# Expert blocks of a mixture-of-experts loop with the weights stationary and the token rows moving

## The chip, the cores and the metric

One core of a Trainium2 chip runs the whole program. The metric is the device time of one execution in microseconds; three runs of the kernel before took 991.32, 992.77 and 993.33 us, median 992.77.

## The reference, cut to what matters

Two decoder layers work on 1,024 tokens of width 256. Each has an attention, a second mixing part and a feed-forward part, and a layer norm behind each. The change touches the feed-forward part of the first layer alone, a mixture of 64 experts with one shared expert that every token passes:

```python
E, K, H, F_EXP = (64, 6, 256, 176)
def _swiglu(x, g, v, o):
    return jax.nn.silu(x @ g) * (x @ v) @ o
scores = jax.nn.softmax(x @ w_router.T, axis=-1)
topw, topi = jax.lax.top_k(scores, K)
combine = jnp.zeros((T, E), x.dtype).at[jnp.arange(T)[:, None], topi].add(topw)
def body(acc, ws):
    g, v, o, cw = ws
    return (acc + cw[:, None] * _swiglu(x, g, v, o), None)
routed, _ = jax.lax.scan(body, jnp.zeros_like(x), (wg, wv, wo, combine.T))
shared = _swiglu(x, swg, swv, swo)
return (routed + shared).reshape(b, s, h)
```

Each token goes to six experts; an expert has 176 hidden units; g and v are 256 x 176, o is 176 x 256, all f32.

## The kernel before, in words

The kernel is written in five instruction streams, one for each engine, that are ordered by semaphores. The first 450 us are the first layer's attention and scan. Then comes routing (471 to 513 us in the profile): the router's logits, the top six of each token, the rank of each token within its expert, and from these a table of blocks. A block is 128 token rows of one expert. Block e is expert e's first 128 rows, for e from 0 to 63; what goes beyond is put into more blocks behind. The blocks are worked in groups of four (NJ). Groups 0 to 15 (FIXED) are always there and their experts are known, so their weights can be loaded ahead; how many more groups are used (one here, 17 in all) comes out of routing, and for these SyncE reads each block's expert number from memory.

In routing the shared expert is worked too, four token tiles of 128 rows at a time: gate and value product, tanh, two multiplies on VectorE, two transposes of the hidden values, ScalarE's copy of them, the down product, a copy into y_sh (lines 948 to 966, 1785 to 1817, 2307 to 2317). Its instructions stand in each engine's order between those of routing.

For a block of the loop the following is done.
- POOL gathers the block's 128 token rows of x from DRAM (an indirect DMA into xg, line 1479), as soon as the rows of the same place in the group before have been turned.
- TensorE turns xg by two transposes (line 1006); ScalarE copies the result into xgT.
- TensorE multiplies: xgT is the stationary operand (128 x 128, once for each half of the width), and the 352 gate and value columns of the expert move (line 948). Out come token rows by hidden units.
- ScalarE takes the tanh of half the gate; VectorE forms (tanh + 1) * gate and multiplies by the value (lines 2310, 2314), which is twice the wanted product.
- TensorE turns the 176 hidden columns in two halves of 88 (line 954), ScalarE copies them into hidT, and TensorE multiplies them with the down weights (line 960), hidT stationary, 256 columns moving.
- VectorE halves the result into y_out (line 2468), SyncE stores it into y_dram (line 651) and then loads the weights of the block two groups on into the place that has come free (lines 630 and 631).

Weights have room for two groups (RING = 2); xg, xgT, hidT and y_out have room for one. Every matmul with f32 operands shows in the trace as two instructions of the same shape, a transpose as one. TensorE's order in a group is: the gate/value products of blocks 0 to 3, with the turns of the hidden values of blocks 0 and 1 among them; then for each block the down product, the turn of the next group's gathered rows, and the turn of the hidden values two blocks on:

```python
for j in range(NJ):
    up_g(j)
    if j >= 2:
        turn_up(j - 2)
for j in range(NJ):
    down(i * NJ + (j + TILES), j, 2 * j + 1, lambda f: dn(j, f))
    turn_g(i + 1, j)
    if j + 2 < NJ:
        turn_up(j + 2)
```

SyncE's order is block by block: wait for the copy of block j, store it, load the weights for the same place. VectorE may overwrite a block's y_out when the store of that place, a group earlier, has landed (semaphore y_stored[j]). Between the expert work VectorE and ScalarE do pieces of the second layer's key preparation (rotate_key, rest, stack, pick_weights and others), one piece in each block's place.

After the loop POOL waits for all stores of y and gathers each token's six rows back from y_dram (line 1507), where slot_idx has the row numbers; VectorE adds them up with the weights of routing. Everything after that is the same in both kernels.

Of the kernel before, what the change touches and what calls it, by code (L numbers as in the profile page):

```python
# [16 lines left out]
P = 128  # L17
# [3 lines left out]
KD = D // P  # L21
# [12 lines left out]
FH = F // 2  # L34
FP = 96
# [99 lines left out]
ACT_STEPS = 1 + PAIRS + 1  # L135

# [18 lines left out]
def build(nc, a, out):  # L155

    with ExitStack() as ctx:
# [180 lines left out]
        g_th = sb("g_th", [P, NJ, F])  # L338
        hid = sb("hid", [P, NJ, F])
        hidT = sb("hidT", [FH, NJ, 2 * P])  # L340
        xg = sb("xg", [P, NJ, D])
        xgT = sb("xgT", [P, NJ, KD * P])
        sh_gv = sb("sh_gv", [P, KD, 2 * F])
        sh_dn = sb("sh_dn", [FH, 2, D])
# [133 lines left out]
        y_stored = [sem(f"y_stored{j}") for j in range(NJ)]  # L478
# [3 lines left out]
        gv_ready = sem("gv_ready")  # L482
        g_tanh = sem("g_tanh")
        g_silu = sem("g_silu")
        hid_ready = sem("hid_ready")
        hid_turned = sem("hid_turned")
        hidT_copied = sem("hidT_copied")
# [57 lines left out]
        def pair(n):  # L545
            return ps[:, n:n + 2, :].rearrange("p a b -> p (a b)")

# [6 lines left out]
        def _(sp):  # L554
# [69 lines left out]
            for dst, src in ((sh_gv, "sh_gv"), (sh_dn, "sh_dn"), (pos, "pos"), (ident_bf, "ident_bf"),  # L624
                             (x_wq, "x_wq"), (x_wo, "x_wo"), (head_sel, "head_sel")):
# [3 lines left out]
            def load_block(e, j, gv, dn):  # L629
                sp.dma_start(gv, a["w_gv"][bass.ds(e, 1)].rearrange("a p k n -> (a p) k n")).then_inc(w_loaded[j], 16)  # L630
                sp.dma_start(dn, a["w_dn"][bass.ds(e, 1)].rearrange("a p k n -> (a p) k n")).then_inc(w_loaded[j], 16)

            for r in range(RING):
                for j in range(NJ):
                    if r:
                        sp.wait_ge(w_loaded[j], 32 * r)
                    load_block(r * NJ + j, j, w_gv[:, r * NJ + j], w_dn[:, r * NJ + j])
# [25 lines left out]
            used = used_groups(sp)  # L663
            with sp.Fori(FIXED, used) as i:
                for j in range(NJ):
                    e = sp.value_load(expert_row[0:1, bass.ds(i * NJ + (j - E), 1)], min_val=0, max_val=E - 1)
                    buf = bass.ds((i & 1) * NJ + j, 1)
                    store_y(i - RING, j)
                    sp.wait_ge(w_loaded[j], at(i, 32, 0))
                    sp.sem_inc(load_due, 1)  # L670
                    load_block(e, j, w_gv[:, buf].rearrange("p a k n -> p (a k) n"),
                               w_dn[:, buf].rearrange("p a k n -> p (a k) n"))
            for r in range(RING):
                for j in range(NJ):
                    store_y(used - RING + r, j)
# [23 lines left out]
        def _(pe):  # L699
# [245 lines left out]
            def gate_up(j, x_of, w):  # L945

                for k in range(KD):
                    last = mm(ps[:, j, 0:2 * F], x_of(k), w(k), start=(k == 0), stop=(k == KD - 1))  # L948
                last.then_inc(gv_ready, 1)

            def turn_hid(n, j, bk):
                pe.wait_ge(hid_ready, n + 1)
                for f in range(2):
                    last = nc.tensor.transpose(ps[0:FH, bk, f * P:(f + 1) * P], hid[:, j, f * FH:(f + 1) * FH], ident[:])
                last.then_inc(hid_turned, 1)

            def down(n, j, bk, w):
                pe.wait_ge(hidT_copied, n + 1)
                for f in range(2):
                    last = mm(ps[:, bk, 256:512], hidT[:, j, f * P:(f + 1) * P], w(f), start=(f == 0), stop=(f == 1))  # L960
                last.then_inc(down_ready, 1)

            def shared_up(tiles):

                for t in tiles:
                    if t >= NJ:
                        pe.wait_ge(down_copied, t - NJ + 1)
                    gate_up(t % NJ, lambda k: xT[:, k, t * P:(t + 1) * P], lambda k: sh_gv[:, k, :])

            def shared_down(tiles):  # L970
                for t in tiles:
                    turn_hid(t, t % NJ, t % NJ)
                for t in tiles:
                    down(t, t % NJ, t % NJ, lambda f: sh_dn[:, f, :])

            pe.wait_ge(layer_loaded, 128)
            shared_up(range(NJ))
# [10 lines left out]
            shared_down(range(NJ))  # L988
            shared_up(range(NJ, TILES))
# [11 lines left out]
            shared_down(range(NJ, TILES))  # L1001

            def turn_g(i, j):
                pe.wait_ge(gathered[j], at(i, 16, 16))
                for k in range(KD):
                    last = nc.tensor.transpose(ps[:, 2 * j, k * P:(k + 1) * P], xg[:, j, k * P:(k + 1) * P], ident[:])  # L1006
                last.then_inc(xg_turned, 1)

            def group(i, gv, dn):
                def up_g(j):  # L1010
                    pe.wait_ge(xgT_copied, at(i, NJ, j + 1))
                    pe.wait_ge(w_loaded[j], at(i, 32, 32))
                    pe.wait_ge(down_copied, at(i, NJ, j + 1) + TILES - NJ)
                    gate_up(2 * j + 1, lambda k: xgT[:, j, k * P:(k + 1) * P], lambda k: gv(j, k))

                def turn_up(j):
                    turn_hid(i * NJ + (j + TILES), j, 2 * j + 1)

                for j in range(NJ):
                    up_g(j)  # L1020
                    if j >= 2:
                        turn_up(j - 2)
                for j in range(NJ):
                    down(i * NJ + (j + TILES), j, 2 * j + 1, lambda f: dn(j, f))
                    turn_g(i + 1, j)
                    if j + 2 < NJ:
                        turn_up(j + 2)

            pe.wait_ge(down_copied, TILES)
# [3 lines left out]
            with pe.Fori(0, FIXED // RING) as d:  # L1033
                for r in range(RING):
                    group(d * RING + r, lambda j, k: w_gv[:, r * NJ + j, k, :], lambda j, f: w_dn[0:FH, r * NJ + j, f, :])
            used = used_groups(pe)
            with pe.Fori(FIXED, used) as i:
                group(i, lambda j, k: w_gv[:, bass.ds((i & 1) * NJ + j, 1), k, :].rearrange("p a n -> p (a n)"),
                      lambda j, f: w_dn[0:FH, bass.ds((i & 1) * NJ + j, 1), f, :].rearrange("p a n -> p (a n)"))

# [4 lines left out]
            pe.wait_ge(down_copied, at(used, NJ, 0) + TILES)  # L1045
            pe.wait_ge(xgT_copied, at(used, NJ, NJ))
# [358 lines left out]
        def _(pool):  # L1405
# [54 lines left out]
            pool.wait_ge(layer_loaded, 128)  # L1460
# [39 lines left out]
            for j in range(NJ):  # L1500
                pool.wait_ge(y_stored[j], at(used, 16, 0))
# [81 lines left out]
        def _(act):  # L1583
# [201 lines left out]
            def g_tanh_of(n, j, bk):  # L1785
                act.wait_ge(gv_ready, n + 1)
                f(g_th[:, j, :], ps[:, bk, 0:F], ACT.Tanh, scale=0.5).then_inc(g_tanh, 1)

            def hidT_of(n, j, bk):
                act.wait_ge(hid_turned, n + 1)  # L1790
                f(hidT[:, j, :], ps[0:FH, bk, 0:2 * P], ACT.Copy).then_inc(hidT_copied, 1)
# [6 lines left out]
            for r in range(TILES // NJ):  # L1798
                for j in range(NJ):
                    g_tanh_of(r * NJ + j, j, j)  # L1800
                if r:
                    for t in range(1, TILES):
                        scale_hot(t)
                    act.wait_ge(angle, 8)
                    f(cos_sin[:], ang[:], ACT.Sin).then_inc(cos_sin_ready, 1)
                    act.wait_ge(route_mm, 3)
                    f(expert_row[:], ps[0:1, Y, 0:P], ACT.Copy).then_inc(route_act, 1)
                else:
# [1061 lines left out]
```

## Time and profile before

| | before |
|---|---|
| runs, us | 991.32, 992.77, 993.33 |
| span of the profiled execution (the page gives no other time of it), us | 985.7 |
| mean granted TensorE clock | 0.961 |
| TensorE busy | 870.2 us, 88% |
| VectorE busy | 720.6 us, 73% |
| ScalarE busy | 510.4 us, 52% |
| POOL busy | 407.1 us, 41% |
| bytes moved by DMA | 106.46 MB |

The span runs from the first to the last instruction. The shares are averages over stages with quite different limits: in the stage of the expert loop the DMA engines, which over the whole span move 108 GB/s, move about 310. A row of a timeline gives start, duration, engine, line, operation and shape of merged instructions, and in brackets the idle time before them. Matmuls are pipelined, so the step from one to the next is shorter than the duration of one. In rows of DMA issues the last figure is the median time from issue to landing.

### The profile page before, as it was taken

What the parts mean: (1) busy time and instruction counts of PE and PEld (TensorE: products, weight loads), DVE (VectorE), ACT (ScalarE), POOL (GpSimd) and SP (SyncE); (2) the same over time, 40 slices, a digit from 0 to 9 for tenths busy, and PEclk for the clock granted to TensorE, in tenths of its full rate; (3) what the DMA queues carried; (4) which work ended last, traced back from release to release, by engine and by line L of the source; (5) the groups of instructions that cost most, each with busy time, mean ns of one, the idle gap of its engine ahead of it and who ended that gap; (6) DMA issues with size and microseconds to landing.
All of it is one profiled execution on the core that took longest, in us unless ns stands there. A gap on an engine that the chain in (4) does not pass through costs nothing.

```text
span 985.7 us, 15418 instructions
## 1 busy us (share of the span) xinstructions
PE 870.2 (88%) x5267; PEld 568.3 (58%) x5271; DVE 720.6 (73%) x1377; ACT 510.4 (52%) x1022; POOL 407.1 (41%) x338
## 2 busy tenths in 40 slices
PE   7999999999999999988889999999546867899886
PEld 3466666666565666656666777677423654343443
DVE  5667786959696867768774556665467798998797
ACT  3563554545544444445444334455522457898485
POOL 0203448494848577534214333333377312221013
PEclk9999999999999999989999999999866998999998
DMA  5451212112131221100926999999633000000001
GB/s 189 153 196 27 65 49 86 70 65 77 58 102 53 81 75 65 44 1 1 238 94 216 298 311 310 313 312 303 179 96 98 26 1 3 5 8 6 1 6 38
DMA packets 54743, 106.46 MB, mean 108 GB/s; under 512 B 8909, under 2 KB 26645, under 8 KB 54165
## 3 DMA queue, kind: packets, MB, share of 16 engines
q1 hardware_dynamic: 48917, 89.88, 29.6%
q0 software_dynamic: 5760, 15.74, 6.0%
q8 instruction: 37, 0.61, 0.3%
q14 instruction: 29, 0.24, 0.1%
HBM read 88.45 MB, written 17.14 MB: 107 GB/s over the span
## 4 chain that ended last, share of the span: by engine, by line
PE 54%; DVE 19%; DMA 10%; issue 5%; ACT 5%; SPq 3%; POOL 3%; DVEq 0%; ACTq 0%; POOLq 0%
PE ps L777 10%; PE ps L715 6%; DMA w_dn<-in_w_dn 5%; PE ps L873 5%; PE ps L725 4%; DVE row_max L2696 3%; PE ps L948 3%; DMA y_dram<-y_out 3%; PE ps L1280 3%; POOL key_part L1507 2%; DVE state L2119 2%; PE ps L795 2%; PE ps L960 2%; DMA key_part<-y_dram,slot_idx 2%; PE ps L1266 2%
## 5 line engine op out<-in xcount | busy, mean ns | idle before, releaser
L1479 POOL DMA_INDIRECT xg<-x_dram,tok_of x68 | 65.1, 958 | 131.8 <-PE ps L1006 94.2
L777 PE MATMUL ps<-w_vg,xT 128*128 128x512 f32 x256 | 116.8, 597 | 1.2 <-DVE th L2162 1.2
L1429 POOL TENSOR_TENSOR state<-state,rows_bc 128x1024 f32<-128x1024 f32 x22 | 53.8, 2446 | 95.5 <-DVE state L2119 41.9
L715 PE MATMUL ps<-xT,w_qks 128*128 128x512 f32 x192 | 86.5, 596 | 5.2 <-ACT qT L1585 5.2
L948 PE MATMUL ps<-w_gv,xgT 128*128 128x352 f32 (+1 forms) x272 | 87.4, 464 | 2.5 <-DMA w_dn<-in_w_dn 2.4
L2696 DVE TENSOR_REDUCE row_max<-ps 128x4 f32<-128x1024 f32 x64 | 74.3, 1217 | 7.1 <-PE ps L1245 6.3
L2130 DVE TENSOR_TENSOR aT<-ps,tri 128x768 f32<-128x768 f32 x64 | 59.7, 954 | 27.0 <-PE ps L725 26.9
L1585 ACT ACTIVATE probT<-ps 128x512 f32<-128x512 f32 x128 | 69.5, 594 | 10.1 <-PE ps L1266 9.6
L777 PEld LDWEIGHTS ps<-w_vg,xT 128*128 128x128 f32 x256 | 45.8, 190 | 48.8 <-issue 43.1
L960 PE MATMUL ps<-w_dn,hidT 88*128 88x256 f32 (+1 forms) x272 | 70.0, 379 | 0.0
L948 PEld LDWEIGHTS ps<-w_gv,xgT 128*128 128x128 f32 x272 | 48.9, 190 | 27.0 <-issue 5.2
L715 PEld LDWEIGHTS ps<-xT,w_qks 128*128 128x128 f32 x192 | 34.9, 190 | 46.6 <-issue 36.4
L1422 POOL TENSOR_TENSOR drive<-du,rows_bc 128x1024 f32<-128x1024 f32 x26 | 61.0, 2361 | 0.1
L1585 ACT ACTIVATE v<-ps 128x256 f32<-128x256 f32 x64 | 24.5, 382 | 70.6 <-PE ps L777 70.3
L1507 POOL DMA_INDIRECT key_part<-y_dram,slot_idx x48 | 49.9, 1039 | 26.9 <-DMA y_dram<-y_out 12.6
L873 PE MATMUL ps<-w_o,oT 128*128 128x256 f32 x256 | 60.7, 386 | 0.3 <-DVE xres L2235 0.3
L2162 DVE SCALAR_TENSOR_TENSOR th<-th,ps 128x256 f32<-128x256 f32 x64 | 26.5, 417 | 44.7 <-ACT th L1585 44.0
L2468 DVE TENSOR_SCALAR y_out<-ps 128x256 f32<-128x256 f32 x68 | 28.7, 422 | 41.7 <-DMA y_dram<-y_out 26.7
L873 PEld LDWEIGHTS ps<-w_o,oT 128*128 128x128 f32 x256 | 48.1, 194 | 9.9 <-issue 4.2
L1433 POOL TENSOR_TENSOR y<-y,state 128x1024 f32<-128x1024 f32 x22 | 51.9, 2357 | 1.7
L1585 ACT ACTIVATE g_th<-ps 128x176 f32<-128x176 f32 x76 | 23.6, 317 | 54.6 <-PE ps L948 54.4
L2310 DVE SCALAR_TENSOR_TENSOR g_th<-g_th,ps 128x176 f32<-128x176 f32 x76 | 25.4, 335 | 35.5 <-ACT g_th L1585 34.7
(327 smaller groups left out, 2066.6 us busy)
## 6 DMA issues: line engine op xcount, KB each, us to landing
w_gv<-in_w_gv SPq DMA_DIRECT2D x68, 352.0 KB, 8.2
rows_bc<-x_dbl_dram SPq DMA_DIRECT2D x32, 512.0 KB, 3.8
w_dn<-in_w_dn SPq DMA_DIRECT2D x68, 192.0 KB, 9.6
y_dram<-y_out SPq DMA_DIRECT2D x68, 128.0 KB, 7.5
y_dram<-blank SPq DMA_DIRECT2D x4, 1408.0 KB, 13.2
w_vg<-in_wvg SPq DMA_DIRECT2D x8, 512.0 KB, 4.9
w_qks<-in_wqks SPq DMA_DIRECT2D x8, 384.0 KB, 3.1
w_o<-in_wo SPq DMA_DIRECT2D x8, 256.0 KB, 2.7
```

What stands on the lines that cost most here:

```text
L715: last = mm(bank(PJ + n % 2), w_qks[:, k, part * P:(part + 1) * P], xT[:, k, half * 512:(half + 1) * 512], start=(k == 0), stop=(k == KD - 1))
L777: last = mm(bank(PJ + t % 2), xT[:, k, t * P:(t + 1) * P], w_vg[:, k, :], start=(k == 0), stop=(k == KD - 1))
L873: last = mm(ps[:, X + b % 2, 256 * t:256 * t + 256], oT[:, h, c:c + P], w_o[:, h, :], start=(h == 0), stop=(h == 1))
L948: last = mm(ps[:, j, 0:2 * F], x_of(k), w(k), start=(k == 0), stop=(k == KD - 1))
L960: last = mm(ps[:, bk, 256:512], hidT[:, j, f * P:(f + 1) * P], w(f), start=(f == 0), stop=(f == 1))
L1422: G.tensor_tensor(drive_buf(m), du[:, e], b_row[:, n % 2], ALU.mult).then_inc(drive_ready, 1)
L1429: G.tensor_tensor(state_of(m), state_of(m), c_row[:, n % 2], ALU.mult).then_inc(read_out, 1)
L1479: G.indirect_dma_start(xg[:, j, :], None, x_dram, bass.IndirectOffsetOnAxis(ap=col, axis=0)).then_inc(gathered[j], 16)
L1507: G.indirect_dma_start(yg[:, n % 8, :], None, y_dram, bass.IndirectOffsetOnAxis(ap=slot_idx[:, n // TOPK, n % TOPK:n % TOPK + 1], axis=0)) ...
L1585: return nc.scalar.activation(out, in_, func, **kw)
L2130: return V.tensor_tensor(aT[:, 2 * b:2 * b + 2, :], ps[:, first_bank:first_bank + 2, 0:384], tri[:].unsqueeze(1).to_broadcast([P, 2, 384]) ...
L2696: V.tensor_reduce(row_max4[:, u, :, 4 * i + 2 * (b % 2):4 * i + 2 * (b % 2) + 2], src, AX.X, ALU.max).then_inc(unit_free, 1)
```

## The change

Gate and value products are turned: the expert's weights become stationary and the 128 token rows of a block move, so the hidden values come out with units on the partitions and tokens along the columns, as the down product needs them. The transposes of the hidden values and ScalarE's copies of them go. The 176 units are split into 112 (FA) and a rest of 64 (FB). For the 112, gate and value are products of their own; the rests of gate and value are one product with 128 columns of weights, gate in partitions 0 to 63 and value in 64 to 127. The multiply puts the rest of an even block into partitions 0 to 63 of hidT_b and that of an odd block into 64 to 127, and their down products, each over 64 rows, stand one behind the other into different banks. ScalarE's Silu takes the place of the tanh and one of VectorE's multiplies; the factor 0.5 goes.

The work of a group goes by pairs of blocks. All four down products are counted as one event; two VectorE copies take the four results (even and odd blocks), then SyncE stores each pair in one DMA with 2 KB for each partition (in y_dram the rows of a pair of blocks lie one in the other, and slot_idx is computed for that by four more operations) and loads the weights of the pair's blocks, three DMAs a block instead of two, without the 8 padded rows of w_dn. The two stores of group 15 are issued by ScalarE; the last stores stand inside the loop instead of behind it. VectorE's copies wait for both stores of the group before. rotate_key moves ahead of the copies. The shared expert is worked in the same turned form, 512 tokens at a time, its last multiplies now ahead of the table's end.

```diff
-        w_gv = sb("w_gv", [P, RING * NJ, KD, 2 * F])
-        w_dn = sb("w_dn", [FP, RING * NJ, 2, D])
+        w_up = sb("w_up", [P, RING * NJ, KD * UP])
+        w_dn = sb("w_dn", [FA, RING * NJ, D])
+        w_low = sb("w_low", [P, RING * NJ // 2, D])
...
+        def y_rows(i, p):
+            rows = y_dram[bass.ds(i * (NJ * P) + p * 2 * P, 2 * P), :]
+            return rows.rearrange("(r two) d -> r (two d)", two=2)
...
@@ SyncE
-            def store_y(i, j):
-                sp.wait_ge(down_copied, at(i, NJ, j + 1) + TILES)
+            def store_y(i, p):
+                sp.wait_ge(down_copied, at(i, 2, COPIED + 2))
                 sp.sem_inc(load_due, 1)
-                sp.dma_start(y_dram[bass.ds(i * (NJ * P) + j * P, P), :], y_out[:, j, :]).then_inc(y_stored[j], 16)
+                sp.dma_start(y_rows(i, p), y_pair(p)).then_inc(y_stored[p], 16)
             with sp.Fori(0, FIXED // RING - 1) as d:
                 for r in range(RING):
-                    for j in range(NJ):
-                        store_y(d * RING + r, j)
-                        sp.wait_ge(w_loaded[j], at(d, 32 * RING, 32 * (r + RING)))
-                        sp.sem_inc(load_due, 1)
-                        load_block(d * (RING * NJ) + ((r + RING) * NJ + j), j, w_gv[:, r * NJ + j], w_dn[:, r * NJ + j])
+                    for p in range(2):
+                        store_y(d * RING + r, p)
+                        for j in (2 * p, 2 * p + 1):
+                            sp.wait_ge(w_loaded[j], at(d, LOADS * RING, LOADS * (r + RING)))
+                            sp.sem_inc(load_due, 1)
+                            load_block(d * (RING * NJ) + ((r + RING) * NJ + j), j, r)
...
@@ TensorE
+                for p in range(2):
+                    pe.wait_ge(xgT_copied, at(i, 2, p + 1))
+                    pe.wait_ge(hid_ready, at(i, 4, HIDDEN - 4 + p + 1))
+                    for o in range(2):
+                        j = 2 * p + o
+                        pe.wait_ge(w_loaded[j], at(i, LOADS, LOADS))
+                        up(ps[0:FA, p, 2 * o * P:(2 * o + 1) * P], w_of(j), "gate", x_of(j))
+                        last = up(ps[0:FA, p, (2 * o + 1) * P:(2 * o + 2) * P], w_of(j), "value", x_of(j))
+                    last.then_inc(up_ready, 1)
+                for p in range(2):
+                    pe.wait_ge(hid_ready, at(i, 4, HIDDEN - 4 + 2 + p + 1))
+                    for o in range(2):
+                        last = up(ps[:, 2 + p, o * P:(o + 1) * P], w_of(2 * p + o), "low", x_of(2 * p + o))
+                    last.then_inc(up_ready, 1)
+                pe.wait_ge(down_copied, at(i, 2, COPIED))
+                for p in range(2):
+                    pe.wait_ge(hid_ready, at(i, 4, HIDDEN + p + 1))
+                    for o in range(2):
+                        mm(ps[:, 4 + o, p * D:(p + 1) * D], hidT_a[:, 2 * p + o, :], w_dn[:, r * NJ + 2 * p + o, :],
+                           start=(p == 0), stop=False, skip_group_check=True)
+                    for o in range(2):
+                        turn_g(i + 1, 2 * p + o)
+                for p in range(2):
+                    pe.wait_ge(hid_ready, at(i, 4, HIDDEN + 2 + p + 1))
+                    for o in range(2):
+                        rows = slice(HIGH * o, HIGH * o + FB)
+                        last = mm(ps[:, 4 + o, p * D:(p + 1) * D], hidT_b[rows, p, :], w_low[rows, r * (NJ // 2) + p, :],
+                                  start=False, stop=True, skip_group_check=True)
+                last.then_inc(down_ready, 1)
...
@@ ScalarE, one group
+                for p in range(2):
+                    act.wait_ge(up_ready, at(i, 4, HIDDEN + p + 1))
+                    f(silu_a[:, 2 * p:2 * p + 2, :], ps[0:FA, p, :].rearrange("p (e two n) -> p e two n", e=2, two=2)[:, :, 0, :],
+                      ACT.Silu).then_inc(silu_ready, 1)
...
@@ VectorE, one group
+                dve.wait_ge(down_ready, at(i, 1, 3))
+                if not first:
+                    for p in range(2):
+                        dve.wait_ge(y_stored[p], at(i, 16, 0))
+                for o in range(2):
+                    V.tensor_copy(y_out[:, o::2, :], bank(4 + o).rearrange("p (a d) -> p a d", a=2)).then_inc(down_copied, 1)
```

## Rows read from the trace of the kernel before

**Rows 1.** Windows by group: us; engines' busy times (PE to POOL); PEclk, DMA share, GB/s

```profile
521.27:531.33 10.06, 10.06 (x50) 7.61 (x50) 3.99 (x12) 5.24 (x14) 4.72 (x6) 1.00 0.32 86
...
582.14:592.64 10.50, 10.28 (x50) 7.43 (x49) 5.51 (x18) 4.00 (x12) 3.78 (x5) 1.00 1.06 317
...
676.74:687.42 10.68, 10.38 (x51) 7.44 (x49) 6.11 (x18) 5.92 (x18) 2.33 (x4) 1.00 1.05 290
```

**Rows 2.** DMA issues of 552 to 675 us

```profile
w_gv<-in_w_gv SPq DMA_DIRECT2D x46, 352.0 KB, 8.4
w_dn<-in_w_dn SPq DMA_DIRECT2D x46, 192.0 KB, 9.7
y_dram<-y_out SPq DMA_DIRECT2D x47, 128.0 KB, 8.2
```

**Rows 3.** Chain that ended last, 455 to 760 us: start, duration, what

```profile
574.02 9.40 DMA y_dram<-y_out
...
699.41 3.57 DMA y_dram<-y_out
```

**Rows 4.** Waits of 521 to 700 us: who for whom, us, times, longest

```profile
DVE y_out L2468 <- DMA y_dram<-y_out: 26.7, 19, 1.9
```

**Rows 5.** Timeline of TensorE, loop's first group

```profile
529.15 1.03 PE L960 MATMUL ps<-w_dn,hidT 88*128 88x256 f32 x4
530.02 0.38 PE L1006 MATMUL ps<-ident,xg 128*128 128x128 f32 x2
```

**Rows 6.** Timeline of TensorE in the attention, 57 to 59.8 us

```profile
56.91 0.39 PE L840 MATMUL ps<-v,aT 128*128 128x128 f32 x2
57.13 0.39 PE L841 MATMUL ps<-v,aT 128*128 128x128 f32 x2
57.45 0.92 PE L725 MATMUL ps<-wT,eT 64*128 64x256 f32 x8
58.30 0.49 PE L839 MATMUL ps<-v,aT 128*128 128x128 f32 x2
```

**Rows 7.** Timeline of SyncE's DMA issues, loop's first burst

```profile
528.28 0.36 SPq L651 DMA_DIRECT2D y_dram<-y_out  x1
...
530.32 0.37 SPq L651 DMA_DIRECT2D y_dram<-y_out  x1
...
534.01 0.36 SPq L651 DMA_DIRECT2D y_dram<-y_out  x1
...
535.17 0.35 SPq L631 DMA_DIRECT2D w_dn<-in_w_dn  x1
```

**Rows 8.** DMA issues at 528.28, 530.32, 534.01 and 535.17, one by one

```profile
y_dram<-y_out SPq DMA_DIRECT2D x1, 128.0 KB, 1.7
...
y_dram<-y_out SPq DMA_DIRECT2D x1, 128.0 KB, 5.5
...
y_dram<-y_out SPq DMA_DIRECT2D x1, 128.0 KB, 6.6
...
w_dn<-in_w_dn SPq DMA_DIRECT2D x1, 192.0 KB, 7.5
```

**Rows 9.** Groups by line and form, whole span

```profile
L2103 DVE TENSOR_SCALAR sT<-ps 128x512 f32<-128x512 f32 x16 | 10.3, 676 | 4.8 <-PE ps L715 4.8
...
L2468 DVE TENSOR_SCALAR y_out<-ps 128x256 f32<-128x256 f32 x68 | 28.7, 422 | 41.7 <-DMA y_dram<-y_out 26.7 <-PE ps L960 14.2
```

**Rows 10.** Timeline of routing, 469 to 523 us

```profile
479.23 5.00 PE L948 MATMUL ps<-sh_gv,xT 128*128 128x352 f32 x16 [0.71 <-DMA x_bo<-in_x_bo]
...
484.66 0.34 DVE L2310 SCALAR_TENSOR_TENSOR g_th<-g_th,ps 128x176 f32<-128x176 f32 x1
...
487.14 0.21 DVE L2367 TENSOR_SCALAR blocks<-ps 128x64 f32<-128x64 f32 x1
```

**Rows 11.** Timeline of SyncE, last group's loads

```profile
677.14 0.36 SPq L651 DMA_DIRECT2D y_dram<-y_out  x1
...
679.71 0.36 SPq L651 DMA_DIRECT2D y_dram<-y_out  x1
```

More of the change, by code:

```diff
@@ L943, in _, with part_of, up @@
             last.then_inc(route_mm, 1)
-            def gate_up(j, x_of, w):
+            def part_of(w, k, part):
+                first = k * UP + dict(gate=0, value=FA, low=2 * FA)[part]
+                return w[:, first:first + (2 * FB if part == "low" else FA)]
+            def up(out, w, part, x_of):
                 for k in range(KD):
[L948 to L960, printed above, removed]
-                last.then_inc(down_ready, 1)
[L963 to L977, printed above, removed]
+                    last = mm(out, part_of(w, k, part), x_of(k), start=(k == 0), stop=(k == KD - 1))
+                return last
+            Y_SH = (3, 2)
+            def shared_up(h):
+                def x_of(k):
+                    return xT[:, k, h * 512:(h + 1) * 512]
+                if h:
+                    pe.wait_ge(hid_ready, 2)
+                up(ps[0:FA, 0, :], sh_up, "gate", x_of)
+                up(ps[0:FA, 1, :], sh_up, "value", x_of).then_inc(up_ready, 1)
+                if h:
+                    pe.wait_ge(down_copied, 2)
+                up(bank(2), sh_up, "low", x_of).then_inc(up_ready, 1)
@@ new lines, in shared_down @@
+            def shared_down(h):
+                pe.wait_ge(hid_ready, 2 * h + 1)
+                if h:
+                    pe.wait_ge(down_copied, 2)
+                for t in (0, 1):
+                    mm(ps[:, Y_SH[0], t * D:(t + 1) * D], hidT_a[:, t, :], sh_dn[:], start=(t == 0),
+                       stop=False, skip_group_check=True)
+                pe.wait_ge(hid_ready, 2 * h + 2)
+                for t in (0, 1):
+                    mm(ps[:, Y_SH[1], t * D:(t + 1) * D], hidT_a[:, 2 + t, :], sh_dn[:], start=(t == 0),
+                       stop=False, skip_group_check=True)
+                for t in (0, 1):
+                    for n in range(2):
+                        rows = slice(HIGH * n, HIGH * n + FB)
+                        last = mm(ps[:, Y_SH[n], t * D:(t + 1) * D], hidT_b[rows, t, :], sh_low[rows, :], start=False,
+                                  stop=True, skip_group_check=True)
+                last.then_inc(down_ready, 1)
@@ L1005, in turn_g @@
                 for k in range(KD):
-                    last = nc.tensor.transpose(ps[:, 2 * j, k * P:(k + 1) * P], xg[:, j, k * P:(k + 1) * P], ident[:])
+                    last = nc.tensor.transpose(ps[:, 6 + j // 2, (j % 2) * D + k * P:(j % 2) * D + (k + 1) * P],
+                                               xg[:, j, k * P:(k + 1) * P], ident[:])
                 last.then_inc(xg_turned, 1)
[L1009 to L1027, printed above, removed]
@@ L1818, in xgT_of @@
-            def xgT_of(i, j, first):
-                act.wait_ge(xg_turned, at(i, NJ, j + 1))
+            nc.scalar.preload_act_table_set("silu_and_others")
+            silu_shared(0)
+            scale_probs()
+            keep_shared(0)
+            scale_hot(0)
+            silu_shared(1)
+            for t in range(1, TILES):
+                scale_hot(t)
+            act.wait_ge(angle, 8)
+            f(cos_sin[:], ang[:], ACT.Sin).then_inc(cos_sin_ready, 1)
+            act.wait_ge(route_mm, 3)
@@ L1840, in cast_key @@
+                for p in range(2):
+                    act.wait_ge(up_ready, at(i, 4, HIDDEN + 2 + p + 1))
+                    f(silu_b[HIGH:P, 2 * p:2 * p + 2, :].rearrange("p a b -> p (a b)"),
+                      ps[0:FB, 2 + p, 0:2 * P], ACT.Silu).then_inc(silu_ready, 1)
+                for p in range(2):
+                    xgT_of(i + 1, p)
+                if side:
+                    side(2)
+                    side(3)
             def cast_key(j, q):
@@ L1857, in stack_key @@
                     last.then_inc(stacked, 1)
-            for j in range(NJ):
-                xgT_of(0, j, True)
+            for p in range(2):
+                xgT_of(0, p, True)
             for i in range(FIXED):
@@ L2362, in _ @@
                                         in1=far_base[:].unsqueeze(1).to_broadcast([P, TILES, E]), op0=ALU.mult, op1=ALU.add))
-            for j in range(NJ):
-                hidden(j, j, j)
+            hidden_shared(0, 0)
+            hidden_shared(0, 1)
             dve.wait_ge(route_mm, 2)
```

236 lines of the change are left out of this document (123 added, 113 removed).

## The prediction

> **What bounds the kernel now.** The page comes first: TensorE is its busiest engine, so shorter matmuls look like a gain. The change touches only routing's shared expert and the loop over 17 groups of four expert blocks, so I then read the loop group by group, in windows cut where a group's first gate matmul starts [rows 1]. It runs from 521.27 to the issue of its last y store at 699.41 [rows 3], 178.1 us. Its first groups take 10.0 with TensorE busy throughout; from 582.14 to 687.42 ten groups take 105.3, 10.53 each, with holes on TensorE and a DMA share of 1.05 to 1.06. The issues of this stretch say what a group moves [rows 2]: a block's weights are 352 + 192 KB, its y 128 KB, its gather by the code 128 rows of 1 KB. Four blocks are 3,200 KB, 3.28 MB; over 10.53 us that is 311 GB/s, the rate that the windows show. Landings of 8 to 10 us after issue say the same: a full queue. The chain of waits runs through one of these landings in most of these groups, such as a y store of 9.40 [rows 3], and VectorE waits 26.7 us in all, 19 times, for a y store before it may overwrite y_out [rows 4]. So after the first groups the DMA queue and the reuse of buffers bound the loop; TensorE is a near second.
>
> **TensorE, part by part.** A f32 matmul is two instructions, a transpose one. Starts give the step of one instruction: four with 256 moving columns take 0.87 to the next line's start, 0.217 each [rows 5]; pairs of 128 columns, each instruction with a new 128-column weight, start 0.22 apart, 0.11 each [rows 6], so the weight loads of the turned form stay hidden. A group before is 10.0 [rows 1]. After: gate, value and rest are 48 x 0.11 = 5.3; down of the 112 units 8 x 0.217 = 1.7; eight transposes of gathered rows 0.9; the eight hid transposes go. The rests' downs take 4 x 0.217 = 0.9 if pairs run side by side. Eight 64-row instructions (four of 256, four of 128 columns) took 0.85 from their start to the next line's; one after the other they need 4 x 0.217 + 4 x 0.11 = 1.31; and entering that form cost 0.1, since the pair before it took 0.32 instead of 0.22 [rows 6]. With 0.2 for in and out the group is 9.0, so 1.0 less. This counts only where TensorE ends last: between 0 and 17 x 1.0. I count it for group 0 alone, because the transfers are late next.
>
> **The transfers.** Weights go from 544 to 352 + 112 + 64 = 528 KB a block (no padded rows); y and gathers keep their bytes. A group is 3.21 MB, 10.33 us at 311 GB/s: 0.2 less. What moves is when they are issued. Before, each block's y is copied, stored and its weights reloaded as soon as its own down product ends: the first store is issued at 528.28, 7.0 after the loop's start [rows 7]. After, all four blocks end together and two copies of 512 columns follow, 0.68 each as for another 512-column read of PSUM [rows 9], 1.5 with handoffs. So the first store and reload come at 9.0 + 1.5 = 10.5, 3.5 later, and then in a burst: store, six loads, store, six loads. SP takes 1.16 from a store to the second load after it and 1.85 a round of store and two loads [rows 7], so 0.69 from a load to the next store, and I take 0.55 for each further load: the second store is issued 1.16 + 4 x 0.55 + 0.69 = 4.05 behind the first, the last load about 8 behind.
>
> Two loops now close over a whole group.
> Stores: the next copies wait until both stores have landed, and the second stands behind two blocks' loads. In the loop's first burst, on an empty queue, the store behind one block landed at 530.32 + 5.5 = 535.8 and the one behind three at 534.01 + 6.6 = 540.6 [rows 7, 8]. Two blocks ahead is between, 538.2, so 9.9 after the burst's first issue. With the copies' 1.4 and 0.35 for handoffs (my allowance) the loop is 11.65.
> Weights, over two groups: that burst's last load landed at 535.17 + 7.5 = 542.7 [rows 7, 8], 14.4 after its first issue, 14.65 with a handoff. The last block's gate and value (0.9), all rests (1.8), downs, turns and rests' downs (3.7) and copies (1.5) follow: 22.5, or 11.25 a group.
> If the queue never empties, its work alone counts: 10.33. So the new period lies between 10.33 and 11.65. I take 10.95, the middle: what is left in the queue at a group's end, and the gathers, cover a part of the burst's start, but not all. Nothing hides this: TensorE's 9.0 ends sooner.
>
> The empty queue's first store landed 1.7 after its issue, the same 128 KB behind one block 5.5 [rows 8]; so here the place in the queue decides. The Trainium skill ("DMA: Bandwidth & Descriptors", section "Anatomy of one DMA — SWDGE (gpsimd) path") gives a DMA a fixed 2.0 us plus bytes / 436e3. By that alone the second store would land 2.6 us after its issue (an estimate from that page), and the store loop would not bind. By that rule the first would land in 2.3 us; it bears the rule out, the second does not.
>
> **Other engines.** ScalarE: four Silu of 256 columns and two copies of 512 take the place of twelve short instructions; VectorE: six multiplies and two copies, of twelve. ScalarE is busy 4.0 and VectorE 5.5 of a window of 10.5 [rows 1]; they stay hidden, or cost up to 0.3 a group where a key step stands ahead of the copies (I take 0). [...] POOL's gathers are issued a little later in the group and needed a group on: 0.
>
> **Routing.** VectorE's eight short products, from 484.66 to the block counts at 487.14 [rows 10], stand ahead of the chain to the first gather, 2.5; three take their place, 0.68 + 2 x 0.42 = 1.5 [rows 9]. Against that the shared gate product, 5.00 on TensorE before [rows 10], becomes 12 instructions of 512 columns (twice 0.217 each, 5.2) and waits for one load more (up to 0.5, an allowance), and the rank products follow it. Bounds: 1.0 gained, 0.7 lost; I take 0.45 gained, since VectorE, not TensorE, ends last there now. The four extra index operations run while VectorE waits for TensorE: 0.
>
> **The end.** For group 16 SP reads each expert's number: 2.57 between two stores [rows 11] instead of 1.85. Its loads are issued within 1.5 + 4 x 2.57 = 11.8 after group 14's copies and land about 4 later (between 1.7 [rows 8] and 9.7 [rows 2], near the low end as little is queued); 7.85 follow, 23.4 in all with no other handoff, where two periods are 21.9. The last store landed 3.57 after its issue [rows 3]; two of 256 KB take 0.8 more.
>
> **Sum.** To the last store's issue: 10.5 + 14 x 10.95 + 23.4 + 0.25 = 187.4 against 178.1: 9.3 more. Routing -0.45, the last store +0.8: +9.65. Of the profiled execution the page gives the span, 985.7; the 7.1 us between it and the median of the runs, 992.77, are taken as unchanged. So 985.7 + 9.65 + 7.1 = 1002.4; forecast 1002.
>
> **Rivals.** (1) Faster: the queue itself gets quicker. y goes out in rows of 2 KB instead of 1 KB and the padding is gone; if the mixture then moves at 325 GB/s (one window has 317 [rows 1]) the period is 9.9 and the end 22.4: 10.5 + 138.6 + 22.4 + 0.25 = 171.8, with the other two terms 6 less, 987. It decides from a period under 10.3. Against it: more, smaller loads in a group, and stores that wait. Its extreme is a loop bound by TensorE, 9.0 a group, some 25 us less; a DMA share of 1.06 speaks against that. (2) No change: the queue never empties, 10.33 a group: 10.5 + 144.6 + 23.4 + 0.25 = 178.8, +1 with the other terms, 994. For it: the queue was full before. By the fixed cost that the Trainium skill gives (the section named above) it would come out so. (3) The store loop in full, 11.65: 10.5 + 163.1 + 23.4 + 0.25 = 197.3, +19.5, 1012. (4) The rests don't run side by side: 0.9 more on TensorE, felt only in the weights loop, at most 0.45 a group, +6 on the forecast, 1008; the 64-row instructions speak against it [rows 6].
>
> **How the numbers follow.** Forecast, a period of 10.6 to 11.3 (997 to 1007): 0.48. Rivals 3 and 4: 0.17. Rival 2 (990 to 997): 0.17. Rival 1: 0.18. Two microseconds, 0.2%, are about what a measurement of this kernel can tell from no change. Faster by more: rival 1 and a little of 2, 0.22; within it 0.12, the middle of 2; slower 0.66. The range 988 to 1014 leaves out the far ends of rivals 1 and 3; the forecast's own range is 997 to 1007.
>
> **What would show it.** Right: the first reload issued near 531, groups starting some 10.9 apart from the second on, VectorE's copies waiting for a y store in nearly every group, TensorE waiting for loads inside groups, under 305 GB/s. Routing right: the first gather 0.3 to 0.6 earlier. Wrong: starts 10.4 apart or less with the DMA share still at 1.06 (rivals 2 and 1); over 9.5 of TensorE in group 0 (the step of 0.11 or the pairs); the second store landing within 3 us of its issue.

## The result, and the profile of the changed kernel

The changed kernel takes 1012.92 us (median of 4 runs, 1005.07 to 1016.87) against 992.05 for the kernel before. The ratio of the fast runs is 1.0247, with a 95% interval of 1.0201 to 1.0294, where the two medians alone would give 1.021. It is slower, as forecast, but by 20.9 us instead of 9.65. The two profiled executions lie further apart, 1013.7 and 985.7 in span; what follows explains that pair, 28.0 us.

All of it lies in the loop over the groups. That ran from 521.27 to 699.41, 178.1 us; now it runs from 521.49 to the issue of its last y store at 728.10, 206.6.

Windows by group (the columns of [rows 1]): a first group, a short one, the long one behind it, two stretches of the long one, and the same work as in the first of these two in another long group, group 6.

```profile
521.49:531.30 9.81, 9.81 (x73) 8.96 (x72) 3.40 (x12) 3.31 (x7) 3.83 (x4) 0.92 0.19 53
555.11:564.24 9.13, 9.13 (x74) 8.28 (x72) 4.68 (x14) 2.72 (x6) 3.86 (x5) 1.00 0.82 232
564.24:578.65 14.41, 11.40 (x74) 10.08 (x72) 4.59 (x14) 2.71 (x6) 3.86 (x5) 0.88 1.00 303
570.50:574.88 4.38, 4.38 (x24) 4.38 (x25) 0.89 (x3) 0.76 (x2) 0.00 (x0) 0.61 1.00 312
574.88:578.65 3.77, 3.77 (x26) 2.91 (x24) 2.08 (x9) 1.57 (x3) 1.94 (x2) 1.00 0.91 270
593.60:596.36 2.76, 2.76 (x25) 2.76 (x26) 0.71 (x2) 0.76 (x2) 0.00 (x0) 1.00 1.07 321
```

The even 10.5 of [rows 1] is gone: short groups (9.13, TensorE busy throughout) alternate with long ones (12.33 to 14.75, and 16.39 for group 14), 23.5 a pair around here. TensorE's own work is the 9.13; the rest of a long group is waiting, and a stretch at clock 0.61. Six of the seven long groups up to group 14 have such a stretch (clock 0.50 to 0.65); in group 6 the clock stays at 1.00. TensorE's timeline in the long group:

```profile
564.24 2.14 PE L977 MATMUL ps<-xgT,w_up 128*112 128x128 f32 x16
568.49 1.10 PE L977 MATMUL ps<-xgT,w_up 128*112 128x128 f32 x8 [2.10 <-DMA w_low<-in_w_low]
570.50 4.55 PE L977 MATMUL ps<-xgT,w_up 128*112 128x128 f32 x24 [0.91 <-DMA w_low<-in_w_low]
574.88 1.03 PE L1075 MATMUL ps<-w_dn,hidT_a 112*128 112x256 f32 x4
...
578.65 1.56 PE L977 MATMUL ps<-xgT,w_up 128*112 128x128 f32 x12
```

Blocks 2 and 3 wait for the last of their three loads. After the second wait 24 instructions take 4.38, 0.18 each, where the first 16 took 2.14, 0.13 each. The chain of waits from there (start, duration, what) shows who is late:

```profile
564.67 5.78 DMA w_low<-in_w_low
570.50 4.55 PE ps L977 x24
...
577.55 1.27 issue
578.82 1.30 DVE y_out L2546 x2
...
580.35 0.36 SPq L671
```

That load was the last of SyncE's burst, which began with a store 7.86 us earlier:

```profile
556.81 0.37 SPq L671 DMA_DIRECT2D y_dram<-y_out  x1
...
561.18 0.37 SPq L671 DMA_DIRECT2D y_dram<-y_out  x1
...
564.67 0.47 SPq L649 DMA_DIRECT2D w_low<-in_w_low  x1
```

From one such burst (556.81) to the next but one (580.35) is a closed cycle of two groups: 13.69 until the last load is in and block 3 starts, 4.38 for its products and the rests, 3.77 for downs, turns and rests' downs, 1.70 for copies and handoffs, 23.54.

Landings show that the queue is no longer full (552 to 675 us, beside [rows 2]); each burst meets a queue that has run down.

```profile
w_up<-in_w_up SPq DMA_DIRECT2D x41, 352.0 KB, 4.1
y_dram<-y_out SPq DMA_DIRECT2D x21, 256.0 KB, 2.9
w_dn<-in_w_dn SPq DMA_DIRECT2D x41, 112.0 KB, 4.3
w_low<-in_w_low SPq DMA_DIRECT2D x42, 64.0 KB, 5.0
```

The waits of 521 to 728 us (beside [rows 4]): the load's wait has become the large one, the store's has shrunk to 7 times, each in a short group.

```profile
PE ps L977 <- DMA w_low<-in_w_low: 28.8, 20, 3.6
...
DVE y_out L2546 <- DMA y_dram<-y_out: 17.4, 7, 3.4
```

At the loop's end (beside [rows 11]) SyncE issues group 16's loads from 700.89 to 709.88; TensorE waits 3.61 for the last of them:

```profile
712.70 1.10 PE L977 MATMUL ps<-xgT,w_up 128*112 128x128 f32 x8 [2.10 <-DMA w_low<-in_w_low]
717.41 4.64 PE L977 MATMUL ps<-xgT,w_up 128*112 128x128 f32 x24 [3.61 <-DMA w_low<-in_w_low]
```

### The profile page after: what moved, and what is told of

It is laid out like the page before. It is cut to its first block, busy times and chain, and to the rows that moved or that the text cites. A ratio compares the mean times of both kernels' runs of the same rounds, so it can differ in the third digit from the quotient of the medians.

```text
span 1013.7 us, 15833 instructions
## 1 busy us (share of the span) xinstructions
PE 871.4 (86%) x5651; PEld 592.9 (58%) x5655; DVE 705.6 (70%) x1303; ACT 484.2 (48%) x900; POOL 407.2 (40%) x338
## 4 chain that ended last, share of the span: by engine, by line
PE 54%; DVE 19%; DMA 7%; issue 6%; SPq 5%; ACT 5%; POOL 4%; DVEq 0%; ACTq 0%; POOLq 0%
PE ps L801 10%; PE ps L739 6%; DMA w_low<-in_w_low 5%; PE ps L897 5%; PE ps L749 4%; PE ps L977 4%; POOL key_part L1564 3%; DVE row_max L2776 3%; PE ps L1337 2%; DVE state L2181 2%; PE ps L819 2%; PE ps L1323 2%; PE ps L1075 2%; SPq L649 1%; PE ps L1302 1%
## 5 line engine op out<-in xcount | busy, mean ns | idle before, releaser
L977 PE MATMUL ps<-xgT,w_up 128*112 128x128 f32 (+1 forms) x816 | 112.2, 299 | 29.0 <-DMA w_low<-in_w_low 28.8
L977 PEld LDWEIGHTS ps<-xgT,w_up 128*112 128x112 f32 (+1 forms) x816 | 104.8, 202 | 38.7 <-DMA w_low<-in_w_low 16.9
L2529 DVE TENSOR_TENSOR hidT_a<-silu_a,ps 112x256 f32<-112x256 f32 x34 | 14.3, 419 | 71.8 <-ACT silu_a L1642 71.8
L1642 ACT ACTIVATE silu_a<-ps 112x256 f32<-112x256 f32 (+1 forms) x36 | 14.2, 395 | 90.4 <-PE ps L977 90.4
L2546 DVE COPY y_out<-ps 128x512 f32<-128x512 f32 x34 | 21.9, 686 | 31.9 <-DMA y_dram<-y_out 17.4
L2181 DVE TENSOR_TENSOR_SCAN state<-decay,drive 128x1024 f32<-128x1024 f32 x18 | 40.7, 2276 | 0.0
```

The source lines that it names most:

```text
L977: last = mm(out, part_of(w, k, part), x_of(k), start=(k == 0), stop=(k == KD - 1))
L1642: return nc.scalar.activation(out, in_, func, **kw)
L2181: V.tensor_tensor_scan(state_of(m), decay[:, m % 2], drive_buf(m), 0.0, ALU.mult, ALU.add).then_inc(scanned, 1)
```

## The experiments

Ratios are to the kernel before, measured on the same chip (987.8 to 988.9 us in these runs). "Loop" is from the first gate product to the issue of the last y store of the profiled run.

**The store loop or the weights loop?** (a_y_two) y_out is held twice, so no copy waits for the stores of the group just before.

```
-        y_out = sb("y_out", [P, NJ, D])
+        y_out = sb("y_out", [P, RING * NJ, D])
...
-                        dve.wait_ge(y_stored[p], at(i, 16, 0))
+                        dve.wait_ge(y_stored[2 * r + p], stored)
```

> The changed kernel with y_out held twice (groups of even and odd number write different halves, each with its own stored-semaphores), so that copies wait for the stores of two groups ago. Theory W (the two-group weights loop sets the period: burst's first issue, 13.4 us until the last load has landed, 4.4 for the last block's products at the low clock, 3.9 for the downs, 1.7 for the copies, 23.5 a pair of groups): VectorE's waits for y stores (17.4 us in 7 groups) go, but they stand in the short groups only, and the time stays within 3 us of the changed kernel's 1012.9. Theory S (my rival 3, the store loop): the period falls from 11.8 towards 10.5 and the time by 12 us or more.

Measured: 1014.09, ratio 1.0261 (1.0211 to 1.0311); loop 204.5. No wait of VectorE for a store is left among the waits; TensorE's wait for loads stands as it was:

```profile
PE ps L978 <- DMA w_low<-in_w_low: 26.4, 21, 3.7
```

The store loop, my rival 3, is out as the bound.

**The same loads, but waited for later** (a_split)**.** Gate and value wait for w_up alone, the downs for w_dn and w_low.

```
-                        pe.wait_ge(w_loaded[j], at(i, LOADS, LOADS))
+                        pe.wait_ge(up_loaded[j], at(i, 16, 16))
...
                     for o in range(2):
+                        pe.wait_ge(w_loaded[2 * p + o], at(i, LOADS, LOADS))
```

> The changed kernel with separate semaphores: gate and value wait for w_up alone, the down products for w_dn and w_low; no load is issued at another time. The last block's w_up is issued 1.05 us before its w_low and lands about 2 earlier. Theory W: the pair of groups gets 1.5 to 2.3 shorter, the kernel 10 to 18 us faster. Theory S or a queue that is slower by itself: within 3 us of 1012.9.

Measured: 999.48, ratio 1.0113 (1.0066 to 1.0160); loop 191.6, 15 less. Nothing leaves earlier and nothing is smaller; only the place of one wait moved. TensorE now waits for w_up, and no longer for w_low:

```profile
PE ps L989 <- DMA w_up<-in_w_up: 22.7, 19, 3.6
...
DVE y_out L2559 <- DMA y_dram<-y_out: 10.7, 8, 2.8
```

**Part of the burst issued earlier** (a_up_early)**.** Besides, SyncE reloads a pair's w_up once its rests are multiplied.

```
+                        sp.wait_ge(up_ready, at(d, 4 * RING, 4 * r + HIDDEN + 2 + p + 1))
+                        for j in (2 * p, 2 * p + 1):
...
+                            load_up(d * (RING * NJ) + ((r + RING) * NJ + j), j, r)
                     for p in range(2):
                         store_y(d * RING + r, p)
```

> As a_split, and SyncE reloads a pair's w_up as soon as that pair's rests are multiplied, some 5 us before the group's copies; stores, w_dn and w_low follow the copies as before. Two thirds of the weights so leave the burst. Theory W: no stall inside groups, the period falls to what the queue's work takes, 10.3 to 10.6 (at most 311 GB/s as before), so 990 to 996, near the kernel before. If the new mixture of transfers is slower by itself (under 290 GB/s whatever its order): a period over 11.1 and 1002 or more.

Measured: 990.8, ratio 1.0030 (1.0004 to 1.0056); loop 176.7, 30 less than the changed kernel's. The time is as expected, the period better: 9.57 over groups 2 to 14. The transfers of 560 to 660 us, and the wait that is left:

```profile
DMA packets 19560, 33.18 MB, mean 332 GB/s; under 512 B 2973, under 2 KB 10305, under 8 KB 19558
```

```profile
DVE y_out L2563 <- DMA y_dram<-y_out: 44.4, 13, 5.2
```

The kernel before, in the same stretch and also at a full queue:

```profile
DMA packets 16948, 31.06 MB, mean 311 GB/s; under 512 B 2420, under 2 KB 7253, under 8 KB 16944
```

The Trainium skill ("DMA: Bandwidth & Descriptors", section "Rules for kernel authors") advises to issue a DMA early and to wait on its semaphore late; these two runs are the two halves of that rule, the late wait worth 15 us of loop and the early issue another 15. In the run times they are 13 and 9 us: in its profile a_up_early's loop begins 3.1 us later than a_split's.

**The clock in the loop** (a_fill, and again a_fill2 beside the unchanged a_again)**.** TensorE gets more to do: six f32 products a group, results unused, ahead of the waits of blocks 2 and 3.

```
+                        for _ in range((0, 0, 2, 4)[j]):
+                            mm(ps[:, 2, 3 * P:4 * P], ident[:], ident[:], start=True, stop=True)
                         pe.wait_ge(w_loaded[j], at(i, LOADS, LOADS))
```

> The changed kernel with six more f32 matmuls of 128 columns a group on TensorE, results unused: two before the wait for block 2's weights and four before that for block 3's, 1.3 us of work a group by 0.109 us an instruction. They stand where TensorE waits anyway (3.4 us in each long group). Theory C (part of W: the wait lowers TensorE's clock, and block 3's products and the rests then run at 0.213 instead of 0.109 us an instruction, 1.7 us in each of 8 long groups): the granted clock stays near 1.0 over the stretch after the wait, that stretch falls from 4.3 to about 2.6, and the kernel gets faster by 6 to 14 us although it does more. If the clock is no part of the loop: no change within 3 us. If TensorE's work bounds the loop: 15 to 22 us slower.

Measured: 1006.06, ratio 1.0191 (1.0138 to 1.0244), an interval that overlaps the changed kernel's. So both ran again, side by side:

> The changed kernel itself once more, to have it beside a_fill2 on one chip: about 1013 again, 2.0 to 2.9% over the kernel before, and in a second profile the same pattern of long and short groups, 23 to 24 us a pair, the last block's gate and value and the rests at half the clock in the long ones.

> a_fill once more (six more f32 matmuls a group in TensorE's waits), because its interval, 1.0138 to 1.0244, overlapped that of the changed kernel. Theory C: 5 to 10 us under a_again, intervals apart. Without the clock in the loop: within 3 us of a_again.

Measured: the changed kernel 1016.03, ratio 1.0248 (1.0199 to 1.0297), with the same alternation; with the added products 1001.58, ratio 1.0139 (1.0109 to 1.0169). More work, and by the ratios 11 us less (14 by the medians), just beyond the 5 to 10 expected; the intervals lie apart. TensorE in a longer group of the first of the two runs, and a window over its last stretch:

```profile
560.15 1.13 PE L977 MATMUL ps<-xgT,w_up 128*112 128x128 f32 x8 [0.41 <-DMA w_low<-in_w_low]
561.11 1.06 PE L1063 MATMUL ps<-ident 128*128 128x128 f32 x8
562.12 2.91 PE L977 MATMUL ps<-xgT,w_up 128*112 128x128 f32 x24
```

```profile
562.12:564.87 2.75, 2.75 (x25) 2.75 (x25) 0.70 (x2) 0.76 (x2) 0.00 (x0) 1.00 1.05 332
```

The 24 instructions that took 4.38 at clock 0.61 take 2.75 at 1.00: 1.6 us that stood on the cycle of 23.54. The filling took the place of idle time; groups now take 10.48 (9.14 and the added 1.3) where nothing is late.

**The burst without the turned products** (b_burst)**.** In the kernel before, stores and reloads of a group are held until its fourth copy.

```
-                sp.wait_ge(down_copied, at(i, NJ, j + 1) + TILES)
+                sp.wait_ge(down_copied, at(i, NJ, NJ) + TILES)
```

> The kernel before with one change: SyncE's stores and reloads of a group all wait until its fourth block is copied, so they leave in one burst as in the changed kernel; matmuls and loads stay. Theory W (release in a burst is what costs): first issue some 5.7 us later, then a two-group loop of about 13.5 us from the first issue to the last load landed and 7.5 from the last block's gate to its copies, plus up to 1.7 for the low clock after the wait: 10.5 to 11.4 a group, 997 to 1010 against some 989 for the kernel before. Rival (the turned products or their twelve loads a group cost it, not the burst): within 3 us of the kernel before.

Measured: 1004.6, ratio 1.0205 (1.0148 to 1.0261); loop 195.6, period 11.31. One line of issue order costs 17 us, with the products of the kernel before: 17.4 us of loop, where the whole change costs 28.5. Which wait closes the cycle differs from my account, though: here the stores' is the larger one (waits of 521 to 717 us), and the rate of 560 to 660 us falls.

```profile
DVE y_out L2468 <- DMA y_dram<-y_out: 39.4, 26, 2.8
PE ps L948 <- DMA w_dn<-in_w_dn: 8.3, 11, 1.3
```

```profile
DMA packets 15695, 28.75 MB, mean 287 GB/s; under 512 B 2253, under 2 KB 6733, under 8 KB 15691
```

**What bounded the kernel before?** (b_two) y_out held twice there. SyncE itself now waits for the last store of the same place before it issues the next.

```
-        y_out = sb("y_out", [P, NJ, D])
+        y_out = sb("y_out", [P, RING * NJ, D])
...
-                    V.tensor_scalar(y_out[:, j, :], ps[:, 2 * j + 1, 256:512], 0.5, None, ALU.mult).then_inc(down_copied, 1)
+                    V.tensor_scalar(y_out[:, r * NJ + j, :], ps[:, 2 * j + 1, 256:512], 0.5, None, ALU.mult).then_inc(down_copied, 1)
```

> The kernel before with y_out held twice, so that copies wait for the stores of two groups ago; matmuls, loads and their order stay. My prediction read the kernel before as bound by the DMA queue's work (3.28 MB a group at 311 GB/s, 10.5 us), with the waits for y stores as its sign. If so: no change, within 3 us, the waits stand at the weights instead. If the 311 was no limit of the queue (a_up_early moved 332 GB/s) and the reuse of y_out was the bound: the period falls from 10.4 towards TensorE's 9.95 to 10.1 and the kernel by 4 to 8 us, the rate rises over 320 GB/s.

Measured: 987.97, ratio 0.9997 (0.9969 to 1.0024). VectorE's store wait of [rows 4] falls from 26.7 to 0.7, SyncE's new one (waits of 521 to 705 us) takes 1.7, and the rate stays:

```profile
DVE y_out L2473 <- DMA y_dram<-y_out: 0.7, 1, 0.7
SPq L655 <- DMA y_dram<-y_out: 1.7, 2, 1.5
```

```profile
DMA packets 16860, 30.81 MB, mean 308 GB/s; under 512 B 2406, under 2 KB 7232, under 8 KB 16856
```

So the prediction read the kernel before rightly: in this order of issue its queue is full at about 310 GB/s, and the reuse of y_out is not a bound of its own.

**Why does a full queue move more in a_up_early?** (a_y1k) Its y rows go back from 2 KB to 1 KB, and slot_idx needs four operations less.

```
-            return rows.rearrange("(r two) d -> r (two d)", two=2)
+            return rows.rearrange("(two r) d -> r two d", two=2)
```

> a_up_early with y stored block by block in rows of 1 KB, as the kernel before did, instead of two blocks' rows side by side, 2 KB. a_up_early's queue moved 336 GB/s at a DMA share of 1.05, the kernel before 311 at the same share. If the longer rows make that difference (my rival 1): the period goes from 9.6 back to 10.0 or more, 997 to 1002. If not: within 3 us of a_up_early's 990.8, and the 311 was not the queue's limit for other reasons.

Measured: 993.84, ratio 1.0083 (1.0050 to 1.0117), 3 us over a_up_early by the medians, 5 by the ratios, with intervals that just touch; period 9.85, not 10.0 or more:

```profile
DMA packets 21121, 31.86 MB, mean 319 GB/s; under 512 B 2835, under 2 KB 14719, under 8 KB 21119
```

An effect of the row length is not shown: a_over, below, has 2 KB rows and the loop of a_up_early up to group 13, and its period is 9.87. Nor does the mixture alone make the difference. The same stretch in the kernel before, a_split, a_up_early and a_over (the last two figures are DMA share and GB/s):

```profile
560.00:660.00 100.00, 97.17 (x456) 70.70 (x454) 61.34 (x173) 44.25 (x127) 36.44 (x39) 1.00 1.06 311
560.00:660.00 100.00, 89.43 (x680) 79.08 (x681) 53.11 (x133) 31.52 (x69) 36.13 (x38) 1.00 1.03 301
560.00:660.00 100.00, 96.96 (x750) 86.43 (x749) 56.50 (x143) 36.38 (x78) 41.87 (x43) 1.00 1.04 332
560.00:660.00 100.00, 96.85 (x751) 86.64 (x750) 57.41 (x145) 35.94 (x78) 39.83 (x41) 1.00 1.01 320
```

a_split moves the same transfers as a_up_early, in the changed kernel's order, and at a share of 1.03 they come to 301 GB/s, less than in the kernel before. So the order of issue matters too. What in the order does it, and what the rest of the mixture adds (no padded rows, smaller loads), was not tried.

**The end of the loop, and a version that beats both** (a_over, a_best)**.** Group 16's loads are split in the same way, and ScalarE stores group 14's y; then y_out is held twice as well.

```
+            sp.wait_ge(up_ready, 4 * (FIXED - 2) + HIDDEN + 4)
             with sp.Fori(FIXED, used) as i:
...
+                    load_up(e, j, 0)
+                sp.wait_ge(down_copied, 2 * (FIXED - 2) + COPIED + 2)
...
+                    load_down(experts[j], j, 0)
```

> As a_up_early, and the last group's w_up is reloaded behind group 14's rests too, its w_dn and w_low behind group 14's copies, ahead of no store of SyncE's (ScalarE issues group 14's y stores, as it did group 15's). In a_up_early group 16 still stalled, 18.7 us from its first gate to the last store's issue, and group 15 12.2. If late loads are the end's cause (W): these two fall to about 11 each and 10, 6 to 9 us less than a_up_early's 990.8, so 982 to 985. If the end is set by the gathers or the copies: within 2 us of it.

> As a_over with y_out held twice: copies wait for the stores of two groups ago. In a_up_early VectorE's copies waited 44.4 us for y stores in 13 groups and in four groups TensorE then waited for VectorE's hidT_a. If that store loop is what is left (S after W is gone): a mean period under 9.4 and 3 to 6 us less than a_over, 976 to 982. If the queue's work, 336 GB/s at a_up_early's 9.55 us a group, is the bound: the same as a_over within 2 us, the waits standing at the loads instead.

Measured: 984.0, ratio 0.9961 (0.9936 to 0.9986), and with y_out held twice 980.73, ratio 0.9917 (0.9884 to 0.9951); the two intervals overlap, so what the second step adds is not shown. In the first, group 16 starts with short waits where a_up_early waited up to 2.99:

```profile
686.09 1.10 PE L993 MATMUL ps<-xgT,w_up 128*112 128x128 f32 x8 [0.34 <-DMA w_up<-in_w_up]
687.88 2.91 PE L993 MATMUL ps<-xgT,w_up 128*112 128x128 f32 x24 [0.69 <-DMA w_up<-in_w_up]
```

The second waits neither for weights nor for stores; the gathers are next, and the period of groups 2 to 14 is 9.81, not the 9.4 expected:

```profile
PE ps L1061 <- DMA xg<-x_dram,tok_of: 7.9, 7, 2.1
```

## Why the prediction was wrong in size

By its own steps, in the profiled pair:

- **The bound before**: right (b_two).
- **TensorE**: right. A group without waits takes 9.13 for a predicted 9.0; steps are 0.109 and 0.215; the rests' pairs start 0.007 apart, and eight take 1.13, so rival 4 is out. Only group 0 is 9.81: it begins at the lower clock level, 0.92 in the mean of its window.
- **The burst**: nearly right. Second store 4.37 behind the first for 4.05, last load 7.86 behind for 8 (the prediction's own steps add up to 7.4); first issue 11.53 into the loop for 10.5. The second store landed some 4.8 after its issue (561.18 to the copies at 565.94), for the prediction's 5.9 (9.9 less 4.05), and not the 2.6 of the formula that it weighs. In the section that it names, the Trainium skill gives that formula for DMAs that GpSimd issues; these are SyncE's, and the kernel before's first one took 1.7 where the formula gives 2.3.
- **Store loop**: wrong as a bound. From one burst's first issue over the stores to the next it measured 10.66 (556.81 to 567.47) for 11.65, less than half of 23.54. Copies wait for a store in 7 groups, not in nearly all, and taking the wait away changed nothing.
- **Weights loop**: the right cycle, sized 22.5 for a measured 23.54. Its landing was 1.0 quicker (13.69 for 14.65), the rest within 0.3. **The step that failed** is its term for the last block's gate and value (0.9) and all rests (1.8): they took 4.38, not 2.7. I had costed the stall as waiting time only, and not that the products behind it run at the lower clock level; that is 0.84 a group. With products at full speed this cycle would have been 21.86, or 10.93 a group. Group 6 shows one: its products kept clock 1.00, and from group 4's copies to its own it took 21.47 (578.82 to 600.29).
- **The period of 10.95** was taken by a second wrong step: "I take 10.95, the middle: what is left in the queue at a group's end, and the gathers, cover a part of the burst's start, but not all." The weights loop is a chain in which each part waits for the one before. By the prediction's own figures it needs 11.25 a group, and no mean with the queue's 10.33 was to be taken; that is 0.3 too little. The quicker landing took back 0.48, which the forecast had not worked out, so that 10.95 lies next to 10.93 is luck. From group 0's copies (531.49) to group 14's (697.17) the period was 11.83, 0.88 more than forecast: 0.3 for the middle, 0.84 for the clock, less 0.48 for the landing, 0.14 for downs and copies, and pairs that were on average a little longer than the one above. Over 14 periods that is 12.4 us.
- **The end**: 28.8 from group 14's copies to group 16's for 23.4, 5.4 more. Group 16's last load lands 7.5 after its issue for my 4, with ScalarE's two stores and four gathers issued around it, and 1.7 goes to the clock again (0.60 from 717.41 to 721.89).
- **Other engines, routing**: within their bounds. VectorE's three shared products and their gaps take 1.61 (484.83 to 486.44) for 1.5, the first gather comes 0.35 earlier for 0.3 to 0.6. The loop's start, 519.9 to 525.1 in the profiles of these kernels, differs by more than that, so the gain in routing is not shown.

First issue 1.0, periods 12.4 and end 5.4 are 18.8 of the 19.2 by which the loop missed its forecast of 187.4. This is the profiled pair, which misses the forecast by 18.4; the medians miss it by 11.2. The profiled execution of the changed kernel took 1015.55, 2.6 over its median. That of the kernel before took some 987.6 (an estimate: time lies about 1.9 over the span in every other run here), 4.5 under its median, so most of the 7.1 that the forecast carried over was only this.

The 1.7 is the stall's second price. In the trace TensorE waits 2.10 and, after 1.1 of work, 0.91; of the 24 instructions behind, 15 then start 0.213 apart, as at 1.2 GHz; 0.109 is the step at 2.4. The Trainium skill ("TensorE: Matmul & The Clock Gate", section "HAM oscillation — how this bites in real kernels") tells of a loop that starts each step cold because it waits for a DMA; the trace agrees (0.61 behind the waits, 1.00 in a short group), and a_fill2 shows what it costs. It is not so behind every wait: in group 6 TensorE waits 1.65 and, after as much work, 1.07, and the clock stays at 1.00.

The figure of rival 3, 1012, came out by luck, not by its store loop. The faster queue of rival 1 was real but out of reach of this order of issue: it shows at 332 GB/s once the burst is broken up, and gives 9.57 a group, where rival 1 had 9.9 at 325.

## What to carry over

When a change lets buffers go all at once instead of one by one, add up the closed cycle from release to release; if that exceeds the queue's and the engine's work, it is the period, and no mean with the others is to be taken. Ask of each stall on TensorE whether the clock falls behind it: here it cost its length and, in all long groups but one, the products behind it at a granted clock of 0.50 to 0.65. Waiting only where data is used, and releasing each buffer at its last use, recovered all of the loss here: 980.7 with the same products, 987.8 for the kernel before beside it.

## What the runs showed of the hardware that I had not expected

- Work added into TensorE's waits made the kernel faster, 1.0139 for 1.0248 of the time before, because the granted clock behind them stayed up (1.00 instead of 0.61 in the windows above; 0.98 for 0.94 from 521.5 to 700 us, a_fill2 and a_again).
- A DMA share of 1.03 to 1.06 stood at 301, 311 and 332 GB/s, and 301 and 332 are the same transfers in two orders of issue (a_split, a_up_early). So the share alone doesn't say what a full queue can move.
- ScalarE's sine at 510.06 and the Silu behind it at 524.20 ran without a table load between them. In the kernel before, the sine and the tanh behind it each had one of 1.28 us (510.53 and 521.72).
